# A fused four-layer transformer kernel: which engine rounds the first network's wide rows

## The reference, cut to what matters

```
def _bitlinear(x, w):
    rms = rsqrt(max(mean(w * w), EPS))
    w_quant = clip(round(w * rms), -1, 1) / rms
    scale = 127 / max(max(|x|, axis=-1), EPS)
    x_quant = clip(round(x * scale), -128, 127) / scale
    return einsum('bsd,fd->bsf', x_quant, w_quant)

x = x + tanh(g_xattn[0]) * scan_mixer(context, layernorm(x))      # a state-space scan over 512 steps, 16 states
h = gelu(_bitlinear(layernorm(x), w1))                            # 512 x 2048 per batch entry: "the wide rows"
x = x + tanh(g_ffn[0])   * _bitlinear(h, w2)
x = x + tanh(g_xattn[1]) * attention(layernorm(x), context)
x = x + tanh(g_ffn[1])   * ffn(layernorm(x), proj1, proj2)        # the second network, float32
```

## Time and profile before

| | |
|---|---|
| median of 3 runs | 975.09 us (974.25 to 976.95) |
| the profiled execution, its own time | 976.27 us |
| its span, first to last instruction | 974.2 us |
| TensorE busy | 824.5 us, 85% |
| VectorE busy | 776.4 us, 80% |
| ScalarE busy | 660.9 us, 68% |
| GpSimd busy | 520.0 us, 53% |
| mean granted TensorE clock | 0.919 of full speed |

### The profile page before, as it was taken

The page is one execution under the profiler, slowest core; times in us unless marked ns, Lnnn a source line. Parts: engine busy times, 40 slices in busy tenths (PEclk is TensorE's granted clock), DMA queues, the critical chain, the costliest instruction groups (busy, mean ns, idle before and its releaser), DMA issues. The chain is left out here.

```text
span 974.2 us, 9381 instructions
## 1 busy us (share of the span) xinstructions
PE 824.5 (85%) x2810; PEld 405.8 (42%) x2810; DVE 776.4 (80%) x905; ACT 660.9 (68%) x984; POOL 520.0 (53%) x461
## 2 busy tenths in 40 slices
PE   6721246799799999999799999998999998898999
PEld 2210012344344344454344444443443444456887
DVE  4589997895889998986899998977889997863333
ACT  4599979573699973774699863773799863624442
POOL 0598785211899883203999881215998871012000
PEclk9755558899899999999899999999899999999999
DMA  8079985001199967301499964301699972201231
GB/s 298 11 142 205 269 202 100 1 1 44 30 201 234 235 145 192 108 2 43 86 212 231 242 140 127 109 1 43 123 225 212 218 164 74 109 1 44 87 108 65
DMA packets 47969, 123.74 MB, mean 127 GB/s; under 512 B 5920, under 2 KB 7072, under 8 KB 47408
## 3 DMA queue, kind: packets, MB, share of 16 engines
q0 software_dynamic: 17280, 62.92, 34.3%
q1 hardware_dynamic: 30640, 60.24, 18.2%
HBM read 56.03 MB, written 4.19 MB: 62 GB/s over the span
## 5 line engine op out<-in xcount | busy, mean ns | idle before, releaser
L1668 POOL TENSOR_TENSOR work<-du,bcast 128x1024 f32<-128x1024 f32 x128 | 352.4, 2780 | 33.8 <-ACT bcast L867 33.2
L1271 DVE TENSOR_TENSOR_SCAN pair<-pair,work 128x512 f32<-128x512 f32 x256 | 299.3, 1215 | 34.4 <-ACT pair L882 28.9
L882 ACT ACTIVATE pair<-dt,a_neg 128x512 f32<-128x512 f32 x256 | 165.8, 682 | 20.2 <-DVE work L1278 17.2
L653 PE MATMUL bank<-stage,ring 128*128 128x512 f32 x384 | 172.9, 593 | 1.5 <-ACT stage L1116 1.5
L1278 DVE TENSOR_TENSOR work<-pair,ccast 128x1024 f32<-128x1024 f32 x128 | 156.8, 1225 | 11.6
L1679 POOL DMA_DIRECT2D u<-work x120 | 130.8, 1090 | 49.0 <-DVE work L1278 20.5
L438 PE MATMUL bank<-xd,pick 128*128 128x512 bf16 x128 | 56.3, 440 | 88.1 <-ACT bcast L867 61.8
L653 PEld LDWEIGHTS bank<-stage,ring 128*128 128x128 f32 x384 | 71.8, 190 | 80.5 <-issue 70.9
L1654 POOL TENSOR_SCALAR fst<-fst 128x1 f32<-128x1 f32 x32 | 9.2, 288 | 166.7 <-DVE fst L1505 166.5
L667 PE MATMUL bank<-ring,stage 128*128 128x512 f32 x192 | 85.6, 594 | 1.7 <-ACT hx L1151 1.7
L438 PEld LDWEIGHTS bank<-xd,pick 128*128 128x128 bf16 x128 | 13.1, 102 | 140.6 <-ACT bcast L867 90.1
(11 more groups left out here) (168 smaller groups left out, 1519.9 us busy)
## 6 DMA issues: line engine op xcount, KB each, us to landing
u<-work POOLq DMA_DIRECT2D x120, 512.0 KB, 6.0
ring<-ffn_dram SPq DMA_DIRECT2D x120, 256.0 KB, 5.0
ring<-ffn_dram SPq DMA_DIRECT2D x16, 512.0 KB, 3.3
xres<-x_dram SPq DMA_DIRECT2D x4, 1024.0 KB, 5.4
stage<-w_dram SPq DMA_DIRECT2D x1, 4096.0 KB, 16.9
stage<-w_dram SPq DMA_DIRECT2D x4, 1024.0 KB, 7.4
out_dram<-stage SPq DMA_DIRECT2D x16, 256.0 KB, 2.1
ctxT<-ctxT_dram SPq DMA_DIRECT2D x4, 512.0 KB, 6.8
```

The costliest lines, as they stand in the source:

```text
L653: last = pe.matmul(banks[2 + f % 2][:], piece(b, f)[:, k * P:(k + 1) * P], xnT[:, k, :], start=k == 0, stop=k == J - 1)
L882: act.activation(pairs[s % DECAYBUFS][:, q, :], dt[:, p * HALF + q, :], ACT.Exp, scale=a_neg[:, p * HALF + q, n:n + 1]).then_inc(s_decay, 1)
L1271: dve.tensor_tensor_scan(pair[:, q, :], pair[:, q, :], rows[:, q, :], 0.0, ALU.mult, ALU.add).then_inc(s_scan, 1)
L1668: pool.tensor_tensor(work[:, s % SCANBUFS, :, :], du[:, p * HALF:(p + 1) * HALF, :], bcast[:, n % 2, :].unsqueeze(1).broadcast_to([P, HALF ...
```

## The change

The roundings of row blocks 0 and 1 leave GpSimd's list and go into VectorE's, each right behind the scale of its block. GpSimd's copy of the function is gone; VectorE's (in `closing` and for blocks 2 and 3 before) is unchanged. It concerns the three middle passes, two instructions in each.

```diff
@@ VectorE @@
             def between(b, m):

                 h_scale(b, 0)
+                h_round(b, 0)
                 h_scale(b, 1)
+                h_round(b, 1)
                 h_quant(b, 0)
                 convolve(m, 0)
                 convolve(m, 1)
@@ GpSimd @@
             def between(b, m):

-                h_round(b, 0)
-                h_round(b, 1)
                 norm(b, 0)
                 norm(b, 1)
...
-            def h_round(b, t):
-                pool.wait_ge(s_hsc, b * T + t + 1)
-                carry_wait(pool, "pool")
-                pool.tensor_scalar(h[t], h[t], fst[:, t, 2:3], MAGIC, ALU.mult, ALU.add).then_inc(s_hr, 1)
```

## The result

The changed kernel took 980.89 us (median of 4 runs, 979.91 to 981.40), the kernel before 975.05 us beside it (974.25 to 976.95). The ratio is 1.0047, 95% interval 1.0027 to 1.0067: slower by 5.8 us at the medians. The forecast was 977.5 us with a range up to 979.8: the kernel is slower, as the sum says, and by more than the sum and the range allow. The new profiled execution took 979.91 us itself, with a span of 978.0 against 974.2.

The account below looks back on a forecast made before the run. VectorE and TensorE were taken as level up to `h_quant(1)`, with no slack behind. Two roundings (2.64 us) less the stall (1.71) gave 0.5 + 0.93 + 0.93 = +2.4 us by pass: 977.5 us, range 975.4 to 979.8.

Parts of the forecast that it names:

- The price of two roundings: On VectorE in each middle pass: 1.32 us per rounding, 2.64 us for two, bounds 2.56 to 2.90.
- the stall that goes: VectorE's first convolution row waits for GpSimd's second rounding; with GpSimd idle its excess of 1.71 us goes.
- TensorE's wait: Before `transpose_h(1)`, waiting for `h_quant(1)`: to grow from 0.15 to about 1.1 us.
- the delay by pass: At `down1(0)` in the three middle passes: 0.5, 0.93 and 0.93 us later.
- its way to the scans: The delay at `down1(0)` was to reach the scans of the next entry by the same amount.
- Rival 2: The long convolution row has its own cause and the stall stays: +7.5 us, 982.6 us; chance 0.05.
- Rival 3: TensorE catches up somewhere in `between`, so the delay is hidden: +0, 975.1 us; chance 0.08.
- the one on the clock: At `down1(3)`: two falls of TensorE's clock in three passes stay unchanged; bound one fall, 1.68 us, either way.
- rival 4: One or more clock falls more, 1.68 us each: 979.2 us with one, 982.5 with three; chance 0.17.
- Rival 4's other cause: The added 1.1 us gap before `transpose_h(1)` would add a clock fall in each pass, 982.5 us with three.

Follow-up runs that it names:

- covered pair: Kernel before and changed kernel, both with step-size products padded to 128 rows and 24 idle products at the scans' heads: 963.38 and 965.65 us.
- padded pair: Kernel before and changed kernel, both with the 16-row step-size products padded to 128 rows by zero weights: 968.31 and 972.34 us.
- bare delay: Kernel before plus an unread maximum over 768 numbers on VectorE in each middle pass, before block 2's rounding: 981.66 us, ratio 1.0048.
- the covers: Step-size products padded to 128 rows plus 24 idle products in TensorE's wait at the scans' heads; on the kernel before 963.38 us, ratio 0.9859.
- the repeat with 12 runs: The changed kernel measured once more, no edit, against the kernel before: 981.07 us against 976.88, ratio 1.0037.
- the split: Kernel before with block 1 rounded on VectorE and block 0 still on GpSimd, without padding or idle products: 977.62 us, ratio 1.0013.
- covered kernel before: Kernel before with step-size products padded to 128 rows and 24 idle products at the scans' heads: 963.38 us, ratio 0.9859.
- covered split: Kernel before with 128-row padding and idle products, block 0 rounded on GpSimd and block 1 on VectorE: 962.90 us.

## Why the prediction came out too low

**What was right.** The price of two roundings (2.64 us), the stall that goes (1.71), TensorE's wait (1.09 against "about 1.1"), the delay by pass (0.50, 0.95, 0.95 against 0.5, 0.93, 0.93) and its way to the scans all came as worked out; in the covered pair and in the padded pair the stretches give it again. Rival 2 (the stall stays) is out by the six rows of 4.56 us. Rival 3 (hidden) is out by the stretches.

**The term that failed** is the one on the clock: "I take the number of falls (two of three) as unchanged", priced at nothing in the sum. In the first pair of profiles it was one more, three of three: 2.4 us of delay and 1.68 us for the second pass's fall are 4.1, and what the executions differ by elsewhere, -0.4, makes their 3.7. The shape was rival 4, one fall more, for which the forecast had 0.17 and 979.2 us. Its ground for an unchanged number was weak. One execution had told two falls of three, and a shift of less than a microsecond per pass was taken as harmless since "nothing in the change favours an escape". Nothing favours a fall either, but a bare delay of 2.2 us with no rounding moved costs 4.8, and the covers take 15.3 us away from that kernel, 12.8 to 13.5 from the kernel before.

The sum also left out the clock's other place, the head of the scans, where TensorE idles 5.4 us and comes back at the lower clock. In the first pair of profiles this cost nothing, since both kernels have it three times alike. In the padded pair, with no fall at `down1(3)`, the medians are still 4.0 us apart for 2.42 of delay; there the low stretch at the third head was shorter in the kernel before (0.79 granted from 675 to 683 us) than in the changed one (0.51 from 676 to 683), and the changed one met one more in the last scans (0.57 from 785 to 789). With the heads covered the distance is 2.3. That fits the heads, but the two distances are too uncertain to prove it.

**Rival 4's other cause**, the added gap of TensorE before `transpose_h(1)`, is not it by itself. The changed kernel waits there 0.58 us in the first pass and 1.09 and 1.10 in the others, with the clock at full speed behind it (3.62 us for `down1` of blocks 1 and 2). Padded and covered, the changed kernel keeps these gaps, and its six stretches are 61.27 or 61.28 us each, with no fall in them. The Trainium skill, page "TensorE: Matmul & The Clock Gate", section "A second HAM failure mode: psum-queue depth-cycling", says that frequent short idles between groups make the clock go back and forth; in these traces no fall came at a gap of 0.6 to 1.3 us, and one of three gaps of 2.20 us had one. Whether a wider gap makes a later fall at the 16-row products more likely was not tested: each delay of this study widens a gap too.

**Profile against median.** The prediction took one execution's two falls for the kernel's. Over the later runs the kernel before had a median of 976.2 to 976.9 us, not 975.1, and single runs from 973.4 to 981.9. A part of the measured 5.8 us is that scatter: the repeat with 12 runs gave 4.2. I read the change as 2.4 us of delay, which is shown, and about 2 us of clock, which is argued: from the bare delay's excess, the granted clock of the runs and the covered pair.

**What stays open** is whether the excess of the clock lies at `down1(3)`, at the heads or in the turnings, and why a delay brings it. The covers show that the 16-row products and the idle gap are what the clock falls at; which delay is favourable was not worked out, and it may differ by run, as the split's two groups suggest. The covers also shorten the opening part, which has 16-row products of its own: the first scan comes at 35.2 us in the covered kernel before and at 38.6 in the kernel before, though at 35.9 to 37.1 in the five other profiles without padding. How much of the 13 us that is was not measured apart.

The fastest kernel of the study is the covered split, 962.90 us, 1.4% under the kernel before (ratio 0.9855, 0.9832 to 0.9878). Nearly all of it comes from the covers; the split's 0.5 us is within the scatter.

## What to carry to other kernels

A stall that goes is worth only what the next engine in line can use: here VectorE stood 1.71 us for GpSimd, but taking the stall away brought the scans forward by only 0.08 us in a pass, and the two roundings of 1.32 us each that came in its place delayed them by up to 0.95. When two kernels differ by microseconds and the single runs by as much, cut both spans at the same instructions of each pass: the change stands in the stretches to 0.01 us, and what is left over is something else. If that is TensorE's clock, hold it up in both kernels before judging the change; here this alone gained 13 us, five times the change's own 2.4.

## What the runs showed of the hardware

- At or right behind eight products over 16 rows (3.7 us) TensorE's clock fell to 1.2 GHz in 14 of 18 passes, although TensorE was busy all the time (4.00 of 4.00 us). The same products with 112 rows of zero weights took the same time and no fall followed, in 24 passes of 24. The Trainium skill, page "TensorE: Matmul & The Clock Gate", says in its list of terms that the clock goes by how busy the engine is; by these runs the busy time that the profile shows does not decide it alone.
- A VectorE instruction with two inputs stood still until GpSimd's rounding had ended (2.46 instead of 0.75 us), and six rows took 6.27 us with that rounding beside them and 4.56 in every variant without it. The rounding began 0.28 us behind VectorE's `h_quant` and took 2.75 us, where block 0's, beside a maximum, took 1.97; that `h_quant` held it is read from this, no run shows it alone. VectorE's maximum, with one input, and GpSimd's rounding ran side by side at their full pace (2.28 and 1.98 us).
- 24 idle matmuls of 5.3 us in a gap where TensorE waits anyway, with the padding, took the kernel from 976.2 to 963.4 us; the product behind the gap took 1.98 us instead of 3.78.
